# Experts' first two weights as the stationary operand, in a routed feed-forward layer on one core

## What is computed

```
for _ in range(2):                                   # LOOPS
    z_norm = rmsnorm(z, norm_w)
    scores = softmax(z_norm @ router_w)              # 8 experts
    topk_vals, topk_idx = top_k(scores, 2)           # each token goes to two experts
    for e in range(8):
        h = silu(z_norm @ w1[e]) * (z_norm @ w3[e])  # D = 256 -> FF = 512
        mixed += cw[:, e] * (h @ w2[e])              # 512 -> 256
    z = z + mixed
```

## Time and profile before

| | us |
|---|---|
| median of 3 runs | 1052.67 (1052.53 to 1054.49) |
| the profiled execution | 1050.72, its span 1049.0 |
| TensorE busy in it | 987.4 (94%) |
| DVE busy | 690.5 (66%) |
| ACT busy | 574.7 (55%) |
| POOL busy | 579.5 (55%) |
| first to last matmul of the expert stage | 350.7 to 1027.5 |

### The profile page before, as it was taken

The page is one execution under the profiler, slowest core; times in us unless marked ns, Lnnn a source line. Parts: engine busy times, 40 slices in busy tenths (PEclk is TensorE's granted clock), DMA queues, the critical chain, the costliest instruction groups (busy, mean ns, idle before and its releaser), DMA issues.

```text
span 1049.0 us, 22711 instructions
## 1 busy us (share of the span) xinstructions
PE 987.4 (94%) x7246; PEld 678.7 (65%) x7246; DVE 690.5 (66%) x1497; ACT 574.7 (55%) x1122; POOL 579.5 (55%) x755
## 2 busy tenths in 40 slices
PE   7999997989999899999999999999999999999991
PEld 5677776668888577665666765666755566666661
DVE  7889987999999454684435557535469433575557
ACT  4578786668888545433335565335574333333333
POOL 3356686866798755444443366443365544455435
PEclk9999999999999999999999999999999999999996
DMA  9921111000000234334346435338434433665573
GB/s 315 370 68 31 38 32 22 1 6 21 15 26 16 67 107 125 87 69 101 91 109 167 132 98 139 88 106 181 112 111 117 96 91 92 170 173 119 143 187 130
DMA packets 153818, 109.26 MB, mean 104 GB/s; under 512 B 100992, under 2 KB 140544, under 8 KB 153728
## 3 DMA queue, kind: packets, MB, share of 16 engines
q1 hardware_dynamic: 140096, 70.82, 26.5%
q0 software_dynamic: 13632, 37.24, 12.0%
HBM read 54.27 MB, written 31.20 MB: 81 GB/s over the span
## 4 chain that ended last, share of the span: by engine, by line
PE 69%; DVE 9%; POOL 7%; DMA 6%; ACT 4%; issue 3%; SPq 0%; another core or an unknown queue 0%; POOLq 0%; ACTq 0%; DVEq 0%
PE psum_s L930 32%; PE psum_o L2336 16%; PE psum_s L2325 6%; DMA arena<-arena 4%; PE psum_s L1758 3%; PE psum_t L1753 2%; PE psum_t L764 2%; PE psum_o L1804 2%; POOL arena L1057 2%; DVE arena L1489 1%; DMA arena<-in_rope 1%; PE psum_o L1799 1%; PE psum_o L1811 1%; PE psum_s L1735 1%; PE psum_t L2300 1%
## 5 line engine op out<-in xcount | busy, mean ns | idle before, releaser
L930 PE MATMUL psum_s<-w_all,arena 128*128 x1704 | 392.0, 380 | 4.6 <-issue 1.9
L1980 POOL DMA_INDIRECT token_rows<-arena,result_row_of_row x142 | 147.1, 1036 | 296.5 <-ACT arena L2089 291.2
L930 PEld LDWEIGHTS psum_s<-w_all,arena 128*128 128x128 f16 x1704 | 157.8, 98 | 185.2 <-issue 10.9
L2336 PE MATMUL psum_o<-w_all,arena 128*128 x1704 | 209.4, 273 | 9.1 <-DVE arena L2264 8.2
L915 DVE SCALAR_TENSOR_TENSOR arena<-psum_s,gate_scale,arena 128x512 f32<-128x512 f32 x142 | 106.5, 750 | 161.1 <-ACT arena L909 80.6
L2336 PEld LDWEIGHTS psum_o<-w_all,arena 128*128 128x128 f16 x1704 | 164.7, 98 | 54.1 <-issue 15.4
L2264 DVE TENSOR_TENSOR arena<-psum_s,arena 128x512 f16<-128x512 f32 x142 | 97.8, 689 | 132.3 <-ACT arena L2082 114.2
L2089 ACT ACTIVATE arena<-psum_o 128x256 f32<-128x256 f32 x142 | 54.3, 383 | 216.8 <-PE psum_o L2336 214.1
L891 POOL DMA_INDIRECT arena<-sorted_rows,token_of_row x142 | 139.9, 986 | 49.3 <-issue 40.2
L909 ACT ACTIVATE arena<-psum_s,silu_scale 128x512 f32<-128x512 f32 x142 | 97.6, 687 | 108.1 <-PE psum_s L930 56.6
L2082 ACT ACTIVATE arena<-psum_s 128x512 f16<-128x512 f32 x142 | 84.7, 597 | 33.1 <-PE psum_s L2325 22.9
(11 more groups left out here) (326 smaller groups left out, 1364.8 us busy)
## 6 DMA issues: line engine op xcount, KB each, us to landing
arena<-token_rows SPq DMA_DIRECT2D x64, 256.0 KB, 3.1
w_all<-in_L_ffn_w SPq DMA_DIRECT2D x24, 512.0 KB, 10.1
sorted_rows<-w_all SPq DMA_DIRECT2D x24, 256.0 KB
out<-x_sb SPq DMA_DIRECT2D x7, 512.0 KB, 3.1
arena<-arena SPq DMA_TRANSPOSE x172, 2.4
arena<-sorted_rows,token_of_row POOLq DMA_INDIRECT x142
token_rows<-arena,result_row_of_row POOLq DMA_INDIRECT x142
x_sb<-in_L_attn_x SPq DMA_DIRECT2D x1, 2048.0 KB, 14.8
```

Source lines behind the costliest of these rows:

```text
L930: last = nc.tensor.matmul(bank, e_xT[:, u, lx * DC + c, :], w_split[:, bass.ds(e * EW + at, FF)], start=(q == 0), stop=(q == 3 * DC - 1))
L1980: nc.gpsimd.indirect_dma_start(rows, bass.IndirectOffsetOnAxis(ap=targets[:, at : at + 1], axis=0), y_row[:, u, :], None).then_inc(s_sent[ ...
L2336: last = nc.tensor.matmul(psum_e, hT[:, lh, c, :], w_split[:, bass.ds(e * EW + at, D)], start=(q == 0), stop=(q == 3 * FC - 1))
```

## The change

In `inner` the operands change sides. A piece of 128 columns of the weight (`f` of four) is now the stationary operand and the turned rows are the moving one, 128 columns: 48 matmuls a tile in place of 12. The result in `psum_a` and `psum_b` then stands with the hidden numbers on the partitions and the tokens along the row, so `silu` and `gate` work element by element as before, on the turned form (`h_all`), and `turn_h` with its four transposes, its bank and its semaphore is gone. `h_hi` and `h_lo` read `h_all` in SBUF. New waits take over what `turn_h` had ordered: m = 0 waits for the silu of the tile before, m = 1 for its gate, and `gate` for `h_lo`. Places in `w_all` are computed in bytes over a byte view (`w_bytes`) and the piece is viewed as float16 afterwards, in `inner` and in `outer`.

```
@@ setup
+        w_bytes = w_all[:, :].bitcast(mybir.dt.uint8)
-        h_row = take(FF)
+        h_all = take(FF)
-        psum_h = psum_s[:, 1024:1536]
-        s_th = sem("h_turned")
@@ gate
             dve.wait_ge(s_silu, s + 1)
-            nc.vector.scalar_tensor_tensor(h_row, psum_b, gate_scale[:, 0:1], silu_a, ALU.mult,
+            if s:
+                dve.wait_ge(s_h_lo, s)
+            nc.vector.scalar_tensor_tensor(h_all, psum_b, gate_scale[:, 0:1], silu_a, ALU.mult,
                                            ALU.mult).then_inc(s_h, 1)
@@ inner
             if m == 0:
                 pe.wait_ge(s_turned[u], 16 * (n // UNROLL + 1))
+                if n:
+                    pe.wait_ge(s_silu, n)
+            elif n:
+                pe.wait_ge(s_h, n)
             bank, signal = ((psum_a, s_a), (psum_b, s_b))[m]
-            for q, (c, lx, lw) in enumerate([(c, a, w) for c in range(DC) for a, w in ((0, 0), (1, 0), (0, 1))]):
-                at = ((m * DC + c) * 2 + lw) * GROUP
-                last = nc.tensor.matmul(bank, e_xT[:, u, lx * DC + c, :], w_split[:, bass.ds(e * EW + at, FF)],
-                                        start=(q == 0), stop=(q == 3 * DC - 1))
+            for f in range(FC):
+                for q, (c, lx, lw) in enumerate([(c, a, w) for c in range(DC) for a, w in ((0, 0), (1, 0), (0, 1))]):
+                    at = ((m * DC + c) * 2 + lw) * GROUP + f * P
+                    last = nc.tensor.matmul(bank[:, f * P : (f + 1) * P], w_bytes[:, bass.ds(e * (2 * EW) + 2 * at, 2 * P)].bitcast(F16),
+                                            e_xT[:, u, lx * DC + c, :], start=(q == 0), stop=(q == 3 * DC - 1))
             last.then_inc(signal, 1)
@@ h_hi
-                act.wait_ge(s_th, s + 1)
-                nc.scalar.activation(hT[:, 0, :, :].rearrange("p c t -> p (c t)"), psum_h, ACT.Copy).then_inc(s_h_hi, 1)
+                act.wait_ge(s_h, s + 1)
+                nc.scalar.activation(hT[:, 0, :, :].rearrange("p c t -> p (c t)"), h_all, ACT.Copy).then_inc(s_h_hi, 1)
@@ h_lo
-                nc.vector.tensor_tensor(hT[:, 1, :, :].rearrange("p c t -> p (c t)"), psum_h,
+                nc.vector.tensor_tensor(hT[:, 1, :, :].rearrange("p c t -> p (c t)"), h_all,
@@ turn_h (removed, with its calls)
-                pe.wait_ge(s_h, n + 1)
-                for c in range(FC):
-                    last = nc.tensor.transpose(psum_h[:, c * P : (c + 1) * P], h_row[:, c * P : (c + 1) * P], ident[:, :])
-                last.then_inc(s_th, 1)
@@ outer
-                    last = nc.tensor.matmul(psum_e, hT[:, lh, c, :], w_split[:, bass.ds(e * EW + at, D)],
+                    last = nc.tensor.matmul(psum_e, hT[:, lh, c, :], w_bytes[:, bass.ds(e * (2 * EW) + 2 * at, 2 * D)].bitcast(F16),
```

More of the change, by code:

```diff
@@ L2319, in beside_end @@
                     logits(pe, B + k - 1, p, p % 2)
-            def turn_h(n):
-                pe.wait_ge(s_h, n + 1)
-                for c in range(FC):
-                    last = nc.tensor.transpose(psum_h[:, c * P : (c + 1) * P], h_row[:, c * P : (c + 1) * P], ident[:, :])
-                last.then_inc(s_th, 1)
             def outer(n, e):
@@ L2344, in _ @@
                     n = FIRST[k] + t
-                    if n:
-                        turn_h(n - 1)
                     e = expert(pe, k, t)
@@ L2356, in _ @@
                     before_e = e
-            turn_h(ALL - 1)
             outer(ALL - 1, before_e)
```

## The result

| | before | after |
|---|---|---|
| median, us | 1052.60 | 1206.29 (1205.88 to 1206.51) |
| ratio | | 1.1456, 95% interval 1.1436 to 1.1476 |
| span of the profiled execution | 1049.0 | 1204.8 |
| first to last matmul of the expert stage | 350.7 to 1027.5 | 351.3 to 1182.8 |

The change costs 14.6%; 1197 was forecast, and the range was 1125 to 1260. All times compared are of executions with a mean granted clock of 0.93 or more; one of the kernel with idle transposes had 0.85, took 1241.23 us and is left out. The medians of the kernel before lie between 1048.3 and 1052.6 on the chips used, so each ratio is taken against the kernel before on the same chip, and differences of a few microseconds between traces of different chips mean nothing.

The account below looks back on a forecast made before the run. The array bounded the kernel before; after the change TensorE's sequencer would, at 5.72 us a tile: 142 x 5.72 + 10 = 822 us for the expert stage against 677, +145, so 1197 us, range 1125 to 1260.

Parts of the forecast that it names:

- The pitch of a register operation: Expert stage, TensorE's sequencer: 0.119 us from one register operation to the next, 40 a tile, 4.76 us.
- The rest of the sequencer's sum: Expert stage, each tile: 0.7 us for reading the expert's number and 0.26 for two wait instructions.
- Rival (1): Expert stage: the array still decides, register operations never starve it; 54 us gained, 999 us; chance 7%.
- rival (2): TensorE's sequencer: register operations start near 0.09 us apart, loss small or none, 1052 to 1125 us; chance 6%.
- rival (3): First two weights: loads and matmuls pair up worse, places coming from registers; at worst 1289 us; chance 4%.
- rival (4): TensorE's clock: falls to 1.2 GHz with the array busy 69%, 7.94 us a tile, 1503 us; chance 3%.
- Rival (5): TensorE's instruction queue: more than twice the instructions a tile come too slowly, about 1295 us; chance 4%.
- The tile with router work: Expert stage: 0.4 us extra for each of 24 tiles, for a wait instruction and the logits' wait for zT; 10 us.
- The lower bound, 1125: Whole kernel: low end of the forecast's own spread, 1125 to 1260 us, said to come from the pitch.
- h_hi and h_lo were taken as equal: ACT and DVE: reading SBUF instead of PSUM keeps 0.60 and 0.69 us, hidden under 5 us of cover; no term.
- 54 us for the array alone: Expert stage, array only: a tile takes 3.97 us against 4.35, 0.38 x 142 = 54 us gained.
- The transposes' 62 us: Expert stage, array: the removed transposes of h, 0.44 us a tile, 62 us in all.

Follow-up runs that it names:

- idle transposes: The changed kernel with four transposes a tile put back on TensorE, their results not used; 1207.72 us, ratio 1.1516.
- the run with one place: The changed kernel with the first two weights' place computed once a tile, so all 48 matmuls read the same 128 columns; 1038.40 us, ratio 0.988.
- the logits' move: The changed kernel with the router's logits (eight matmuls on zT) one tile later on TensorE; 1194.82 us, ratio 1.1398.
- 0.17 us for each place (three matmuls): The changed kernel with the first two weights' low halves never addressed, one register operation ahead of three matmuls; 1065.02 us, ratio 1.0127.
- fixed places: The changed kernel with the first two weights' places always those of expert 0, no register operation among the 48 matmuls; 1040.65 us, ratio 0.990.
- 32 loaded places: The changed kernel with the first two weights' 32 places read from an SBUF table by one load a tile, not computed; 1316.51 us, ratio 1.2515.

## Why the prediction was right

Step by step, against the profile after:

- The pitch of a register operation, 0.119 from the earlier trace rows, was measured as 0.120. The operation is 32 ns long and not 36 as the row of L1807 had it, and the price is the mean gap: 0.113 us as a rule and more at about every eighth. The forecast's own 0.129 for the longer operation was such a mean too (0.130 over the kernel before, 0.124 the usual gap).
- The rest of the sequencer's sum, 0.96 us, was 0.1 too high: 0.65 us from the load of the number to the first place where 0.7 stood, and 0.105 for each wait where 0.13 stood. The 40 operations came to 4.8 us where 4.76 stood. The tile, 5.72 us, was 5.70, in small part because these two differences offset each other.
- Rival (1), the array alone, is refuted by the run with one place (168 us fall with the operations and nothing else) and by the idle transposes (62 us of array work for nothing); rival (2), a short pitch, by the pitch itself; rival (3), loads and matmuls that pair up worse than 0.055, by the 2.68 us for 48 in the run with one place; rival (4) by the granted clock of 9 in the page's row for all slices but the last. Rival (5), that so many instructions come too slowly, is refuted as an effect of their number by the idle transposes: 1128 instructions more and a stage 1 us shorter. Whether the longer gap at about every eighth operation, 35 us in all, has to do with how instructions come isn't shown.
- The tile with router work was under-priced: 0.4 us over a bare one, 0.63 measured, 24 x 0.23 = 6 us. Of the 0.63, 0.45 is one wait, as the logits' move shows (6.33 to 5.88 us); I had named the wait and given it too little.
- Sum: 142 x 5.72 + 10 = 822 for the stage was 831.8. Of the 10 us missed 6 are the router's; the rest is the spread over bare tiles, whose mean is 5.74 and median 5.70.
- The lower bound, 1125, has no working in the prediction: the short pitch of 0.09 gives 1052, and a pitch of 0.106 would give 1125. The measured time is far from it, so nothing hangs on it.
- h_hi and h_lo were taken as equal on SBUF and PSUM. The medians are 0.62 us against 0.60 and 0.69 against 0.69, with single h_lo of up to 1.23 us; under the cover of over 5 us it made no difference.
- What was wrong is a number that the forecast didn't need: 54 us for the array alone. The step that failed took the earlier trace rows for every tile. But the bare tiles of the kernel before have a mean of 4.57 and a median of 4.36, 117 x 0.21 = 25 us of tiles that something else held up, and with register operations out of the way the mean fell by only 0.10: the stage gained 12 to 17 us. The prediction had no term for such tiles. In the changed kernel they are 117 x 0.04 = 5 us, since the longer tile covers most of these waits, and so the sum held without the term.
- The transposes' 62 us were counted as removed from the array and hence as nothing in the total. That is what the idle transposes show.

## What to carry to other kernels

Before cutting a matmul with a place from a register into smaller ones, count the register operations against the array time of what stands between them: here one each 0.12 us, and about 0.9 us more a tile for the expert's number and the waits, so anything under 0.12 us of array work for each place starves the array. With 0.17 us for each place (three matmuls) the kernel was still 24 us slower than with fixed places. Count also how far the sequencer can get ahead, here 17 pairs of load and matmul, before a long instruction of its own. TensorE's busy share doesn't show any of it; look for idle time put down to "issue", and for the starts of the sequencer's own instructions at an even pitch. And an engine that has just become faster than its neighbours gives back only what the tiles where it was alone contain.

## What the runs showed of the hardware

- A register operation on TensorE's queue costs 0.113 us as a rule and 0.120 on average, with one or with two loads and matmuls behind it (31 of them over 3.6 us), although it is 32 ns long. The instruction that computes the place in elements is 46 ns long and has a usual gap of 0.124 us, and 40 of them a tile are 61 us more in all.
- A wait that stands as an instruction of its own on TensorE's queue costs 0.105 us (0.76 against 0.65 us from the load of the number to the first place, with it and without).
- A load with its address in a register is as fast as a fixed one: 0.056 us for each pair of load and matmul of 128 columns.
- One instruction can load 32 registers from SBUF: 2.39 us, and 0.59 for 8, 0.30 for 1.
- The sequencer got 17 pairs of load and matmul ahead of the array and no more: in the run with 32 loaded places in all of 105 tiles without other work between, at either clock, and in 100 of 105 in the run with one place (in the others, which had waited, fewer stood ahead).
- The granted clock held at 1.00 in the changed kernel with the array idle for some 30% of a bare tile (1 - 3.99 / 5.70, by the run with one place), in many short holes:

```profile
350.00:800.00 450.00, 429.64 (x4871) 362.68 (x4871) 196.58 (x427) 164.89 (x340) 186.10 (x187) 1.00 0.37 93
```

  In the run with loaded places, where the idle time is one hole of 2.2 us in each tile of 6.1 us, the clock went down again and again (0.50 over 3.2 us in the rows above, 0.957 over the whole run). 0.50 is the lower of the two levels, 1.2 GHz, and 1.00 the higher, 2.4 GHz. Part of that run's loss is this and was not separated.
